# All six key copies of the head preparation on GpSimd, in a kernel of eight chained sublayers

## The chip, the cores and the metric

One core of one Trainium2 chip runs the whole program in one launch. The time is the device time of that core in microseconds. Before the change its median is 3116.63 us over three runs, from 3113.25 to 3116.71.

## The reference

The input is 2 x 1024 tokens of width 128. Four layers follow, each an attention part and a feed-forward part, and around each part there is a layer norm before, a layer norm after and a residual add. The change touches the second part only, `_L0_ffn_ref`, which is 16-head attention of head width 8 plus a mixture of eight experts:

```
qkv = (x @ W_qkv + b_qkv).reshape(B, S, 3, H, hd)          # H = 16, hd = 8, S = 1024
q, k, v = (qkv[:, :, 0], qkv[:, :, 1], qkv[:, :, 2])
attn = jnp.einsum('bqhd,bkhd->bhqk', q, k) / jnp.sqrt(jnp.asarray(hd, x.dtype))
attn = jax.nn.softmax(attn, axis=-1)
attn_out = jnp.einsum('bhqk,bkhd->bqhd', attn, v).reshape(B, S, D)
gate = jax.nn.softmax(x @ W_gate + b_gate, axis=-1)
...
return attn_out + moe_out
```

## The kernel before

The program is a row of phases, one behind another. Each phase is a block with one instruction list for each engine, and engines meet only at semaphores inside a block and at its end. The eight sublayers run in order, with a norm phase between them.

The part concerned is the phase `hprep` (lines 727 to 838), which prepares the 16-head attention of width 8. It works on 16 tiles (g = 0 to 15) of 128 tokens. To get products of float32 quality from bf16 operands, every query and key is split into three bf16 parts: `split3` (L703) casts to `hi`, subtracts, casts to `mid`, subtracts, casts to `lo`. These are five DVE instructions, L705 to L709, and each waits on the one before it through the semaphore `chain`. Keys go into `kstack`, where each head has 64 slots; six of its blocks of eight hold the parts in the order hi, mid, hi, mid, lo, hi. Queries go into `qstack` in another order. Then `kstack` is turned, so that head width lies on partitions.

For each tile the engines do this:

- TensorE (PE): the projection of tile g into one of two PSUM banks (L768, waits until DVE has read tile g-2 from that bank), then `turn(g-2)`: eight transposes of `kstack` (L755), which wait for `stack_act`, `stack_pool`, `stack_dve` and, through `turn_kept`, for ACT to have emptied the same half of the PSUM tile.
- DVE: bias added to q and k (L821, reads PSUM and `bias`) and to v (L823, the same), the five steps of `split3`, then `sem_inc(parts_done)`, which releases ACT and GpSimd. Then DVE itself copies the last three of the six key blocks into `kstack` (L837).
- GpSimd (POOL): the first three of the six key blocks (L805), after `parts_done` and after the transposes of the tile two back.
- ACT: six copies of query parts into `qstack` (L781), then for the tile two back the move of the turned keys from PSUM into `kT` (L786).

`kstack`, `qk`, `parts` and both PSUM tiles have two buffers, taken in turn. `rest` has one. The order on each engine is the order in which the code is written; there is no planner. After `hprep` the phase `heads` (L840 on) computes scores, softmax and values of the same attention; it begins once all engines have left `hprep`.

Of the kernel before, what the change touches and what calls it, by code (L numbers as in the profile page):

```python
# [23 lines left out]
P = 128  # L24
# [341 lines left out]
def load_weights(sp, m, dram, s):  # L366

    if s < len(PACKS):
        at = s % 2 * WPART[0]
        sp.dma_start(m.weights[:, at:at + WIDTHS[s]], dram[f"w{s}"]).then_inc(m.wsem[s], 16)  # L370
# [326 lines left out]

SLOTS = 64
BUFS = 10
POOL_SLOTS = 3  # L700


def split3(nc, chain, src, hi, mid, lo, rest):  # L703

    chain.step(nc.vector.tensor_copy(hi, src))  # L705
    chain.step(nc.vector.tensor_tensor(rest, src, hi, ALU.subtract))
    chain.step(nc.vector.tensor_copy(mid, rest))
    chain.step(nc.vector.tensor_tensor(rest, rest, mid, ALU.subtract))
    chain.step(nc.vector.tensor_copy(lo, rest))  # L709


def small_head_attention(nc, m, dram, s, router):
# [7 lines left out]
    with ExitStack() as keep:  # L720
# [6 lines left out]
        with Phase(nc, "hprep") as ph:  # L727
            kstack = ph.sb("kstack", [P, 2, 16, SLOTS], BF16)
            qk = ph.sb("qk", [P, 2, 256])
            parts = ph.sb("parts", [P, 2, 3, 256], BF16)  # L730
            rest = ph.sb("rest", [P, 256])
            bias = ph.sb("bias", [P, 384])
            proj = ph.ps("proj", 2)
            turned = ph.ctx.enter_context(nc.psum_tensor("hprep_turned", [P, 2, 1024], BF16))
            cleared, proj_done, qk_done, v_done, parts_done, chain_sem, stack_act, stack_pool, stack_dve, turn_done, turn_kept, bias_done, bias_kept = (
                ph.sem(x) for x in ("cleared", "proj_done", "qk_done", "v_done", "parts_done", "chain", "stack_act",
                                    "stack_pool", "stack_dve", "turn_done", "turn_kept", "bias_done", "bias_kept"))
            block = ph.block()

            @block.sync  # L740
            def _(sp):
                load_weights(sp, m, dram, s + 1)

            @block.tensor
            def _(pe):
                pe.wait_ge(m.wsem[s], 16)

                def turn(g):
                    pe.wait_ge(stack_act, g + 1)
                    pe.wait_ge(stack_pool, g + 1)  # L750
                    pe.wait_ge(stack_dve, g + 1)
                    if g >= 2:
                        pe.wait_ge(turn_kept, g - 1)
                    for c in range(8):
                        last = nc.tensor.transpose(turned[:, g % 2, c * P:(c + 1) * P],  # L755
                                                   kstack[:, g % 2, 2 * c:2 * c + 2, :].rearrange("p h d -> p (h d)"),
                                                   m.identb[:])
                    last.then_inc(turn_done, 1)

                nc.tensor.matmul(proj[:, 1, 0:384], m.ones[0:1, :], w["bqkv"], start=True,  # L760
                                 stop=True).then_inc(bias_done, 1)
                for g in range(NT):
                    if g == 1:
                        pe.wait_ge(bias_kept, 1)
                    if g >= 2:
                        pe.wait_ge(qk_done, g - 1)
                        pe.wait_ge(v_done, g - 1)
                    nc.tensor.matmul(proj[:, g % 2, 0:384], m.HT[:, g * P:(g + 1) * P], w["Wqkv"], start=True,  # L768
                                     stop=True).then_inc(proj_done, 1)
                    if g >= 2:  # L770
                        turn(g - 2)
                turn(NT - 2)
                turn(NT - 1)

            @block.scalar
            def _(act):
                def stack(g):
                    act.wait_ge(parts_done, g + 1)
                    hi, mid, lo = (parts[:, g % 2, k, 0:P].rearrange("p (h d) -> p h d", h=16) for k in range(3))
                    for slot, part in enumerate((hi, hi, mid, mid, hi, lo)):  # L780
                        last = nc.scalar.activation(qstack[:, g, :, 8 * slot:8 * slot + 8], part, ACT.Copy)  # L781
                    last.then_inc(stack_act, 1)

                def keep_turned(g):
                    act.wait_ge(turn_done, g + 1)
                    nc.scalar.activation(kT[:, :, g * P:(g + 1) * P], turned[:, g % 2, :].rearrange("p (c n) -> p c n", c=8),  # L786
                                         ACT.Copy).then_inc(turn_kept, 1)
                act.wait_ge(cleared, 5)
                for g in range(NT):
                    stack(g)  # L790
                    if g >= 2:
                        keep_turned(g - 2)
                keep_turned(NT - 2)
                keep_turned(NT - 1)

            @block.gpsimd
            def _(pool):
                pool.wait_ge(cleared, 5)
                for g in range(NT):
                    pool.wait_ge(parts_done, g + 1)  # L800
                    if g >= 2:
                        pool.wait_ge(turn_done, g - 1)
                    hi, mid, lo = (parts[:, g % 2, k, P:2 * P].rearrange("p (h d) -> p h d", h=16) for k in range(3))
                    for slot, part in enumerate((hi, mid, hi, mid, lo, hi)[:POOL_SLOTS]):
                        last = nc.gpsimd.tensor_copy(kstack[:, g % 2, :, 8 * slot:8 * slot + 8], part)  # L805
                    last.then_inc(stack_pool, 1)

            @block.vector
            def _(dve):
                chain = Chain(dve, chain_sem)  # L810
                nc.vector.memset(kstack[:, :, :, 51:64], 0.0).then_inc(cleared, 1)
                nc.vector.memset(kstack[:, :, :, 48:51], 1.0).then_inc(cleared, 1)
                nc.vector.memset(qstack[:, 0:8, :, 48:64], 0.0).then_inc(cleared, 1)
                nc.vector.memset(qstack[:, 8:16, :, 48:64], 0.0).then_inc(cleared, 1)
                nc.vector.memset(vaug[:, :, :, 8], 1.0).then_inc(cleared, 1)
                dve.wait_ge(bias_done, 1)
                nc.vector.tensor_copy(bias[:], proj[:, 1, 0:384]).then_inc(bias_kept, 1)
                dve.wait_ge(bias_kept, 1)
                for g in range(NT):
                    dve.wait_ge(proj_done, g + 1)  # L820
                    nc.vector.tensor_tensor(qk[:, g % 2, :], proj[:, g % 2, 0:256], bias[:, 0:256],  # L821
                                            ALU.add).then_inc(qk_done, 1)
                    nc.vector.tensor_tensor(vaug[:, g, :, 0:8], proj[:, g % 2, 256:384].rearrange("p (h d) -> p h d", h=16),  # L823
                                            bias[:, 256:384].rearrange("p (h d) -> p h d", h=16),
                                            ALU.add).then_inc(v_done, 1)
                    dve.wait_ge(qk_done, g + 1)
                    if g >= 2:
                        dve.wait_ge(stack_act, g - 1)
                        dve.wait_ge(stack_pool, g - 1)
                    split3(nc, chain, qk[:, g % 2, :], parts[:, g % 2, 0, :], parts[:, g % 2, 1, :],  # L830
                           parts[:, g % 2, 2, :], rest[:])
                    dve.sem_inc(parts_done, 1)
                    if g >= 2:
                        dve.wait_ge(turn_done, g - 1)
                    hi, mid, lo = (parts[:, g % 2, k, P:2 * P].rearrange("p (h d) -> p h d", h=16) for k in range(3))
                    for slot, part in list(enumerate((hi, mid, hi, mid, lo, hi)))[POOL_SLOTS:]:
                        last = nc.vector.tensor_copy(kstack[:, g % 2, :, 8 * slot:8 * slot + 8], part)  # L837
                    last.then_inc(stack_dve, 1)

        with Phase(nc, "heads") as ph:  # L840
            qT = ph.sb("qT", [P, 2, 8, P], BF16)
# [49 lines left out]
            slot = {e: k % 2 for k, e in enumerate(RING)}  # L891
# [366 lines left out]
def attention_and_top2(nc, m, dram, s):  # L1258
    with ExitStack() as keep:
        router = Router(nc, keep)  # L1260
        small_head_attention(nc, m, dram, s, router)
        top2_experts(nc, m, dram, s, router)
# [2610 lines left out]
```

## Time and profile before

| | |
|---|---|
| median of three runs | 3116.63 us |
| the profiled execution, its own time | 3116.61 us |
| span of its trace | 3114.8 us |
| stretch from 238 to 287 us (nearly all of the 16 tiles of `hprep`) | 49 us |
| in it DVE busy | 44.38 us |
| in it PE busy | 32.11 us |
| in it ACT busy | 32.09 us |
| in it POOL busy | 11.79 us |

The profile shows one execution. The span runs from its first to its last recorded instruction; 1.81 us of the run lie outside it. A row of the timeline gives the start in us, the time from start to end in us, the engine, the line, the operation with output and input, how many instructions are merged in the row, and in brackets how long the engine had stood idle and who released it. Instructions of one engine that do not wait for each other overlap in the records, so three of 0.29 us can take 0.76 us together. The profile of a kernel of 3 ms must be read by stage: `hprep` is 1.6% of it.

### The profile page before, as it was taken

The numbers are of one execution on the slowest core, as the hardware profiler recorded it, in microseconds if no ns is written. First come the engines' busy times: TensorE is split into PE (matmuls) and PEld (weight loads), VectorE is DVE, ScalarE is ACT, GpSimd is POOL, SyncE is SP. The second block draws the span as 40 slices with busy tenths as digits, with TensorE's granted clock in tenths as the row PEclk, the third lists the DMA queues.
The fourth block names the chain that finished last, engine by engine and source line by source line (L and its number), as shares of the span: only waits on it lengthen the run. The fifth ranks groups of instructions, "written<-read, shape, count | busy, mean of one in ns | idle before, by whom it ended". The sixth has DMA issues, their size and how long they took to land. (4 is left out here: it accounts for less than half of the span.)

```text
span 3114.8 us, 55189 instructions
## 1 busy us (share of the span) xinstructions
PE 2705.1 (87%) x21256; PEld 1691.7 (54%) x21276; DVE 2057.1 (66%) x4308; ACT 1571.8 (50%) x3080; POOL 1074.1 (34%) x784
## 2 busy tenths in 40 slices
PE   8995899989899799998999798798877899777698
PEld 5552455567676566665567566465643334335465
DVE  5758999945644665647554665466548999996554
ACT  4334688862423444444544555365457676643122
POOL 3201000001143344434443444154227777773000
PEclk9995899989899899999999899998999999998899
DMA  1000000001120200000000000000013344340000
GB/s 55 1 4 1 2 3 3 3 2 61 49 92 22 84 1 1 1 1 1 1 1 1 29 1 1 1 1 1 1 52 135 136 143 143 137 141 27 1 1 14
DMA packets 34228, 105.41 MB, mean 34 GB/s; under 512 B 3456, under 2 KB 14592, under 8 KB 33200
## 3 DMA queue, kind: packets, MB, share of 16 engines
q1 hardware_dynamic: 31952, 97.69, 9.0%
q0 software_dynamic: 2016, 4.19, 0.4%
q8 instruction: 171, 2.80, 0.4%
q14 instruction: 89, 0.73, 0.1%
HBM read 94.01 MB, written 7.86 MB: 33 GB/s over the span
## 5 line engine op out<-in xcount | busy, mean ns | idle before, releaser
L2082 POOL TENSOR_TENSOR many_probs<-many_probs,many_rinv 128x2048 f32<-128x2048 f32 (+7 forms) x128 | 269.8, 2107 | 371.6 <-DVE many_rinv L2121 371.6
L1062 DVE TENSOR_REDUCE heads_halfmax<-heads_qmajor 128x1 f32<-128x512 f32 x512 | 316.4, 681 | 32.8 <-PE heads_qmajor L923 29.4
L3477 DVE TENSOR_TENSOR_SCAN stream_state<-stream_decay,stream_state 128x512 f32<-128x512 f32 x256 | 306.3, 1233 | 0.8 <-ACT stream_decay L3309 0.5
L1027 ACT ACTIVATE weights<-heads_kmajor 128x1024 f32<-128x1024 f32 x256 | 259.3, 1027 | 71.7 <-PE heads_kmajor L935 66.3
L2051 ACT ACTIVATE many_probs<-many_score,many_negmax 128x1024 f32<-128x1024 f32 (+7 forms) x256 | 187.4, 737 | 179.7 <-DVE many_negmax L2105 175.9
L2105 DVE TENSOR_REDUCE many_negmax<-many_score 128x1 f32<-128x1024 f32 (+7 forms) x256 | 184.4, 751 | 110.4 <-PE many_score L1980 108.9
L3147 PE MATMUL stream_yacc<-stream_state,ident 128*128 128x512 f32 x512 | 249.1, 614 | 0.4 <-POOL stream_state L3439 0.4
L3309 ACT ACTIVATE stream_decay<-weights,mamba_negA 128x512 f32<-128x512 f32 x256 | 173.0, 689 | 112.5 <-DVE stream_state L3477 111.3
L3439 POOL TENSOR_TENSOR stream_state<-XN,stream_state 128x1024 f32<-128x1024 f32 x85 | 200.4, 2360 | 81.4 <-DVE stream_state L3477 81.1
L1988 PE MATMUL many_ring<-ident,many_probs 128*128 128x128 f32 x1152 | 177.4, 282 | 28.1 <-POOL many_probs L2082 6.5
L3468 DVE TENSOR_TENSOR stream_state<-stream_bspread,stream_du 128x1024 f32<-128x1024 f32 x128 | 153.2, 1197 | 46.5 <-POOL stream_du L3415 38.6
L2041 ACT ACTIVATE many_probsT<-many_ring 128x512 f32<-128x512 f32 x192 | 107.7, 561 | 143.8 <-PE many_ring L1988 143.6
L1988 PEld LDWEIGHTS many_ring<-ident,many_probs 128*128 128x128 f32 x1152 | 127.4, 142 | 91.9 <-DVE many_zT L2115 34.7
L951 PE MATMUL heads_outp<-weights,heads_vaug 128*9 128x128 f32 x4096 | 161.2, 276 | 13.5 <-ACT heads_outT L1020 13.2
L2004 PE MATMUL many_ring<-many_probsT,many_v 128*64 128x128 f32 x2304 | 154.1, 278 | 13.8 <-ACT many_probsT L2041 12.2
L2467 ACT ACTIVATE local_probs<-local_score,local_negmax,loc_norms 128x192 f32<-128x192 f32 x256 | 127.3, 507 | 68.0 <-DVE local_negmax L2482 67.9
L1976 PE MATMUL many_score<-many_kT,many_qT 64*128 64x512 f32 (+3 forms) x768 | 159.8, 520 | 1.2 <-ACT many_probs L2051 1.2
L3147 PEld LDWEIGHTS stream_yacc<-stream_state,ident 128*128 128x128 f32 x512 | 101.2, 198 | 90.0 <-issue 71.8
L3138 PE MATMUL stream_bspread<-stream_BC,stream_select 128*128 128x512 bf16 x236 | 76.2, 399 | 81.8 <-DVE stream_state L3468 74.2
L2004 PEld LDWEIGHTS many_ring<-many_probsT,many_v 128*64 128x64 f32 x2304 | 123.2, 137 | 33.9 <-ACT many_probsT L2041 20.2
L2519 POOL TENSOR_TENSOR local_probs<-local_probs,local_rowsum 128x768 f32<-128x768 f32 x64 | 93.9, 1467 | 137.3 <-DVE local_rowsum L2488 137.3
L184 POOL TENSOR_TENSOR norm_rstd<-norm_rstd,neghalf 128x4 f32<-128x4 f32 x46 | 46.8, 1016 | 263.7 <-DVE norm_rstd L178 263.7
(585 smaller groups left out, 6023.7 us busy)
## 6 DMA issues: line engine op xcount, KB each, us to landing
XN<-mamba_crows SPq DMA_DIRECT2D x85, 512.0 KB, 3.6
stream_crow<-mamba_crows SPq DMA_DIRECT2D x43, 512.0 KB, 3.6
weights<-in_w_dram SPq DMA_DIRECT2D x1, 6148.0 KB, 17.8
weights<-in_w_dram SPq DMA_DIRECT2D x1, 4274.0 KB, 12.8
weights<-in_w_dram SPq DMA_DIRECT2D x1, 3296.0 KB, 10.7
swiglu_pairs<-swiglu_fetched SPq DMA_DIRECT2D x1, 2310.0 KB, 10.2
weights<-in_w_dram SPq DMA_DIRECT2D x1, 2112.0 KB, 7.9
swiglu_fetched<-swiglu_pairs SPq DMA_DIRECT2D x4, 528.0 KB, 7.3
```

The lines of the kernel that those rows point to most:

```text
L951: last = nc.tensor.matmul(outp[32 * j:32 * j + 9, 0, c * P:(c + 1) * P], vaug[:, b * TPB + kc, 4 * c + j, :], probs_of(4 * q + j // 2 * 2 ...
L1027: nc.scalar.activation(probs_of(k).rearrange("p (a n) -> p a n", a=2), kmajor[:, at:at + 2, :], ACT.Exp, scale=SC).then_inc(exp_done, 1)
L1062: nc.vector.tensor_reduce(halfmax[:, g % 2, at, h % 2:h % 2 + 1], qmajor[:, (2 * n + j) % 3, :], AX, ALU.max).then_inc(max_done, 1)
L1988: last = nc.tensor.transpose(ring[:, k % 2, x % 4 * P:(x % 4 + 1) * P], probs[:, n % 4, x * P:(x + 1) * P], m.ident[:])
L2004: last = nc.tensor.matmul(ring[DH * h:DH * (h + 1), k % 2, 0:P], v[:, g % 2, kb, DH * h:DH * (h + 1)], probsT[:, n % 2, x * P:(x + 1) * P] ...
L2051: nc.scalar.activation(probs[:, n % 4, h * wide:(h + 1) * wide], score_of(n, h)[:, 0:wide], ACT.Exp, bias=negmax[:, n % 3, h:h + 1], accum ...
L2082: nc.gpsimd.tensor_tensor(pair, pair, rinv[:, n % 4, :].unsqueeze(2).broadcast_to([P, 2, wide]), ALU.mult).then_inc(norm_done, 1)
L2105: nc.vector.tensor_reduce(negmax[:, n % 3, h:h + 1], score_of(n, h)[:, 0:(UNITS[n][1] + 1) * P], AX, ALU.max, negate=True).then_inc(negmax ...
L3147: last = nc.tensor.matmul(yacc[:, half, :], m.ident[:], state[:, g % STATES, part(half)], start=(g % NS == 0), stop=(g % NS == NS - 1))
L3309: nc.scalar.activation(decay[:, h % DECAYS, :], delta_of(j, ch)[:, part(half)], ACT.Exp, scale=negA[:, a:a + 1]).then_inc(dec_done, 1)
L3439: nc.gpsimd.tensor_tensor(state[:, g % STATES, :], crow_of(g), state[:, g % STATES, :], ALU.mult).then_inc(hc_done, 1)
L3477: nc.vector.tensor_tensor_scan(h[:, part(half)], decay[:, (2 * g + half) % DECAYS, :], h[:, part(half)], 0.0 if half == 0 else h[:, BANK - ...
```

## The change

All six key blocks are copied by GpSimd. DVE goes from `sem_inc(parts_done)` straight to the next tile. The semaphore `stack_dve`, PE's wait for it and DVE's wait for `turn_done` go with the DVE copies.

```
--- before.py
+++ after.py
@@ -697,7 +697,6 @@
 
 SLOTS = 64
 BUFS = 10
-POOL_SLOTS = 3
 
 
 def split3(nc, chain, src, hi, mid, lo, rest):
@@ -732,9 +731,9 @@
             bias = ph.sb("bias", [P, 384])
             proj = ph.ps("proj", 2)
             turned = ph.ctx.enter_context(nc.psum_tensor("hprep_turned", [P, 2, 1024], BF16))
-            cleared, proj_done, qk_done, v_done, parts_done, chain_sem, stack_act, stack_pool, stack_dve, turn_done, turn_kept, bias_done, bias_kept = (
+            cleared, proj_done, qk_done, v_done, parts_done, chain_sem, stack_act, stack_pool, turn_done, turn_kept, bias_done, bias_kept = (
                 ph.sem(x) for x in ("cleared", "proj_done", "qk_done", "v_done", "parts_done", "chain", "stack_act",
-                                    "stack_pool", "stack_dve", "turn_done", "turn_kept", "bias_done", "bias_kept"))
+                                    "stack_pool", "turn_done", "turn_kept", "bias_done", "bias_kept"))
             block = ph.block()
 
             @block.sync
@@ -748,7 +747,6 @@
                 def turn(g):
                     pe.wait_ge(stack_act, g + 1)
                     pe.wait_ge(stack_pool, g + 1)
-                    pe.wait_ge(stack_dve, g + 1)
                     if g >= 2:
                         pe.wait_ge(turn_kept, g - 1)
                     for c in range(8):
@@ -801,7 +799,7 @@
                     if g >= 2:
                         pool.wait_ge(turn_done, g - 1)
                     hi, mid, lo = (parts[:, g % 2, k, P:2 * P].rearrange("p (h d) -> p h d", h=16) for k in range(3))
-                    for slot, part in enumerate((hi, mid, hi, mid, lo, hi)[:POOL_SLOTS]):
+                    for slot, part in enumerate((hi, mid, hi, mid, lo, hi)):
                         last = nc.gpsimd.tensor_copy(kstack[:, g % 2, :, 8 * slot:8 * slot + 8], part)
                     last.then_inc(stack_pool, 1)
 
@@ -830,12 +828,6 @@
                     split3(nc, chain, qk[:, g % 2, :], parts[:, g % 2, 0, :], parts[:, g % 2, 1, :],
                            parts[:, g % 2, 2, :], rest[:])
                     dve.sem_inc(parts_done, 1)
-                    if g >= 2:
-                        dve.wait_ge(turn_done, g - 1)
-                    hi, mid, lo = (parts[:, g % 2, k, P:2 * P].rearrange("p (h d) -> p h d", h=16) for k in range(3))
-                    for slot, part in list(enumerate((hi, mid, hi, mid, lo, hi)))[POOL_SLOTS:]:
-                        last = nc.vector.tensor_copy(kstack[:, g % 2, :, 8 * slot:8 * slot + 8], part)
-                    last.then_inc(stack_dve, 1)
 
         with Phase(nc, "heads") as ph:
             qT = ph.sb("qT", [P, 2, 8, P], BF16)
```

What GpSimd's list holds per tile is afterwards: wait `parts_done`, wait `turn_done` (from the third tile on), six copies, of which the last signals `stack_pool`. Nothing else in the program is changed.

## Rows read from the trace of the kernel before

**Rows 1.** The page: span, and busy time of each engine with share and count.
```profile
span 3114.8 us, 55189 instructions
PE 2705.1 (87%) x21256; PEld 1691.7 (54%) x21276; DVE 2057.1 (66%) x4308; ACT 1571.8 (50%) x3080; POOL 1074.1 (34%) x784
```

**Rows 2.** Stretch, length, busy (count) of PE, PEld, DVE, ACT, POOL; clock, DMA share, GB/s.
```profile
238.00:287.00 49.00, 32.11 (x146) 17.57 (x146) 44.38 (x151) 32.09 (x109) 11.79 (x47) 0.53 0.00 1
```

**Rows 3.** Timeline, DVE, one steady tile, to the next tile's first instruction.
```profile
260.68 0.41 DVE L821 TENSOR_TENSOR hprep_qk<-hprep_proj,hprep_bias 128x256 f32<-128x256 f32 x1
...
261.21 0.28 DVE L705 CAST hprep_parts<-hprep_qk 128x256 bf16<-128x256 f32 x1
261.52 0.43 DVE L706 TENSOR_TENSOR hprep_rest<-hprep_qk,hprep_parts 128x256 f32<-128x256 f32 x1
261.98 0.29 DVE L707 CAST hprep_parts<-hprep_rest 128x256 bf16<-128x256 f32 x1
262.31 0.43 DVE L708 TENSOR_TENSOR hprep_rest<-hprep_rest,hprep_parts 128x256 f32<-128x256 f32 x1
262.77 0.29 DVE L709 CAST hprep_parts<-hprep_rest 128x256 bf16<-128x256 f32 x1
263.21 0.79 DVE L837 COPY hprep_kstack<-hprep_parts 128x128 bf16<-128x128 bf16 x3
263.91 0.41 DVE L821 TENSOR_TENSOR hprep_qk<-hprep_proj,hprep_bias 128x256 f32<-128x256 f32 x1
```

**Rows 4.** Timeline, the other engines in the same tile.
```profile
259.92 1.30 ACT L781 ACTIVATE heads_qstack<-hprep_parts 128x128 bf16<-128x128 bf16 x6 [1.02 <-DVEq L832]
261.13 1.00 ACT L786 ACTIVATE heads_kT<-hprep_turned 128x1024 bf16<-128x1024 bf16 x1
...
263.18 0.76 POOL L805 COPY hprep_kstack<-hprep_parts 128x128 bf16<-128x128 bf16 x3 [2.47 <-DVEq L832]
...
262.28 1.01 PE L755 MATMUL hprep_turned<-identb,hprep_kstack 128*128 128x128 bf16 x8 [0.84 <-ACT heads_kT L786]
263.08 1.59 PE L768 MATMUL hprep_proj<-weights,HT 128*128 128x384 f32 x2
```

**Rows 5.** Timeline, first tile's hand-over, and end of the phase.
```profile
237.51 0.63 DVE L837 COPY hprep_kstack<-hprep_parts 128x128 bf16<-128x128 bf16 x3
237.56 0.76 POOL L805 COPY hprep_kstack<-hprep_parts 128x128 bf16<-128x128 bf16 x3 [10.49 <-DVEq L832]
238.05 0.41 DVE L821 TENSOR_TENSOR hprep_qk<-hprep_proj,hprep_bias 128x256 f32<-128x256 f32 x1
...
285.79 1.30 ACT L781 ACTIVATE heads_qstack<-hprep_parts 128x128 bf16<-128x128 bf16 x6 [1.02 <-DVEq L832]
...
288.14 1.01 PE L755 MATMUL hprep_turned<-identb,hprep_kstack 128*128 128x128 bf16 x8 [2.22 <-ACT heads_kT L786]
```

**Rows 6.** Copies into `kstack`, whole trace: shortest, median and longest in ns.
```profile
L837 DVE COPY hprep_kstack<-hprep_parts x48: 194/320/321, 237.5 to 286.3; 128x128 bf16<-128x128 bf16 x48
L805 POOL COPY hprep_kstack<-hprep_parts x48: 288/293/295, 237.6 to 286.3; 128x128 bf16<-128x128 bf16 x48
```

**Rows 7.** Timeline of the first sublayer, DVE and POOL beside each other.
```profile
57.22 2.36 POOL L607 TENSOR_TENSOR lin_keytotal<-lin_keytotal,lin_key 128x1024 f32<-128x1024 f32 x1 [2.36 <-DVE lin_key L623]
59.01 1.12 DVE L628 SCALAR_TENSOR_TENSOR lin_qry<-lin_featexp,lin_featrelu 128x512 f32<-128x512 f32 x1 [1.87 <-ACT lin_featrelu L577]
61.14 0.69 DVE L628 SCALAR_TENSOR_TENSOR lin_qry<-lin_featexp,lin_featrelu 128x512 f32<-128x512 f32 x1 [0.42 <-ACT lin_featrelu L577]
...
138.31 0.88 DVE L212 TENSOR_TENSOR X<-X,XN 128x128 f32<-128x128 f32 x4
138.47 2.94 POOL L607 TENSOR_TENSOR lin_keytotal<-lin_keytotal,lin_key 128x1024 f32<-128x1024 f32 x1 [2.63 <-DVE lin_key L623]
```

**Rows 8.** Timeline of the Mamba stage, POOL and DVE beside each other.
```profile
2398.12 2.36 POOL L3439 TENSOR_TENSOR stream_state<-XN,stream_state 128x1024 f32<-128x1024 f32 x1 [1.06 <-DVE stream_state L3477]
2399.01 1.20 DVE L3468 TENSOR_TENSOR stream_state<-stream_bspread,stream_du 128x1024 f32<-128x1024 f32 x1
```

More of the change, by code:

```diff
@@ L699 @@
 BUFS = 10
-POOL_SLOTS = 3
 def split3(nc, chain, src, hi, mid, lo, rest):
@@ L734, in small_head_attention @@
             turned = ph.ctx.enter_context(nc.psum_tensor("hprep_turned", [P, 2, 1024], BF16))
-            cleared, proj_done, qk_done, v_done, parts_done, chain_sem, stack_act, stack_pool, stack_dve, turn_done, turn_kept, bias_done, bias_kept = (
+            cleared, proj_done, qk_done, v_done, parts_done, chain_sem, stack_act, stack_pool, turn_done, turn_kept, bias_done, bias_kept = (
                 ph.sem(x) for x in ("cleared", "proj_done", "qk_done", "v_done", "parts_done", "chain", "stack_act",
-                                    "stack_pool", "stack_dve", "turn_done", "turn_kept", "bias_done", "bias_kept"))
+                                    "stack_pool", "turn_done", "turn_kept", "bias_done", "bias_kept"))
             block = ph.block()
@@ L750, in turn @@
                     pe.wait_ge(stack_pool, g + 1)
-                    pe.wait_ge(stack_dve, g + 1)
                     if g >= 2:
@@ L803, in _ @@
                     hi, mid, lo = (parts[:, g % 2, k, P:2 * P].rearrange("p (h d) -> p h d", h=16) for k in range(3))
-                    for slot, part in enumerate((hi, mid, hi, mid, lo, hi)[:POOL_SLOTS]):
+                    for slot, part in enumerate((hi, mid, hi, mid, lo, hi)):
                         last = nc.gpsimd.tensor_copy(kstack[:, g % 2, :, 8 * slot:8 * slot + 8], part)
@@ L832, in _ @@
                     dve.sem_inc(parts_done, 1)
[L833 to L838, printed above, removed]
         with Phase(nc, "heads") as ph:
```

## The prediction

> **What bounds the kernel now.** The page comes first. PE is busy for 87% of the span, DVE for 66%, POOL for 34% [rows 1]. That would make PE the limit and a change on DVE worthless, but it is an average over eight sublayers with different limits. So the second look goes to the stage that is changed. From 238 to 287 us DVE is busy for 44.38 of 49 us, PE and ACT for 32.1 each, POOL for 11.8 [rows 2]. Here DVE is the limit, and POOL has three quarters of its time free.
>
> The third look is the timeline, to see whether DVE ever waits for another engine. One tile takes from 260.68 to 263.91, that is 3.23 us, and in it DVE has no idle time that a row names [rows 3]. ACT waits 1.02 us in each tile and POOL 2.47 us, both for DVE's `parts_done` [rows 4]. PE waits 0.84 us for ACT [rows 4], and ACT waited for DVE. The loop from tile to tile is thus DVE's own instruction list: two bias adds, five dependent steps, three copies.
>
> **What is removed.** The three copies L837 start at 263.21 and the next tile's L821 at 263.91: 0.70 us of DVE's list per tile [rows 3]. In the first hand-over it is 238.05 - 237.51 = 0.54 us [rows 5]. There are 15 hand-overs between 16 tiles. After the last tile nothing on DVE follows, and what ends the phase is ACT and PE, below. If nothing else moved, the gain would be 14 x 0.70 + 0.54 = 10.3 us, with 3.23 - 0.70 = 2.53 us per tile. DVE's wait for `turn_done` and PE's wait for `stack_dve` go too; both hang on work that other waits already cover (POOL waits for the same `turn_done`, PE for `stack_pool`), so I count them at nothing.
>
> **What is added on POOL.** Three copies take 0.76 us and one alone 0.293, so they start 0.235 us apart [rows 4, 6]. Six take 0.293 + 5 x 0.235 = 1.47 us. POOL has 3.23 - 0.76 = 2.47 us free now and would still have 1 us free at 2.53 us per tile. Behind the copies on POOL's queue there are only the next tile's copies.
>
> **Who waits for POOL's last copy.** `turn(g)` on PE does. I set time 0 at the DVE instruction that follows `sem_inc` (263.21 in the trace). POOL starts at -0.03 and would end at 1.44. ACT starts `stack(g)` at -0.06; in the trace its keep of tile g-2 begins 261.13 - 259.92 = 1.21 us later and takes 1.00, so it ends at 2.15. PE starts 0.15 us after that (262.13 to 262.28), at 2.30 [rows 4]. So the transposes wait for ACT's `turn_kept` anyway, and POOL may be 0.8 us later than 1.44 before anybody sees it.
>
> **What is late next.** PE needs 263.08 - 262.28 = 0.80 us for the transposes and 1.59 us for the projection: 2.39 us per tile [rows 4], at a granted clock of 0.53 in this stretch [rows 2]. ACT needs 1.21 + 1.00 = 2.21 us [rows 4]. Both lie under 2.53. The projection for tile g+3 ends at 2.30 + 0.80 + 1.59 = 4.69, and DVE asks for it at two tiles, 5.06. It is in time by 0.37 us. If PE lost the 0.15 us of its hand-over in every tile, its loop would be 2.54 us; this costs 0.01 us a tile. DVE stays the limit, with PE close behind.
>
> **The collision.** This is the term that isn't plain. POOL's copies used to run beside DVE's own copies. Now they run beside the next tile's L821, L823, L705, L706, L707. Does DVE slow down beside POOL? The trace has cases.
> - L837 took 194 ns at the shortest, 320 in the median [rows 6]. The short ones are in the first tile, where DVE started 0.05 us ahead of POOL [rows 5]. In the later tiles POOL starts 0.03 us ahead (263.18, 263.21) [rows 3, 4], and each DVE copy takes 0.126 us longer. POOL's stay at 288 to 295 ns.
> - A DVE instruction with two SBUF inputs, L628, starts at 59.01 beside a POOL instruction that ends at 57.22 + 2.36 = 59.58. It takes 1.12 us in place of 0.69, so its work began at 60.13 - 0.69 = 59.44, which is 0.14 us before POOL's record ends [rows 7].
> - The other way round, POOL's L607 at 138.47 takes 2.94 us in place of 2.36. It was held until 139.05, and the DVE instructions beside it end at 138.31 + 0.88 = 139.19, again 0.14 us later [rows 7].
> - A DVE instruction that reads PSUM and SBUF, L3468, runs in the middle of a POOL instruction, from 2399.01 within 2398.12 to 2400.48, and is done at 2400.21, before POOL's ends [rows 8]. It can't have been held off. L821 and L823 are of that kind.
>
> So I read it as exclusion: each holds the other off from its start until 0.14 us before its record ends. For a POOL copy this is 0.293 - 0.14 = 0.153 us. A DVE copy that starts 0.03 us later should wait 0.12, and 0.126 was measured.
>
> The Trainium skill (SBUF — State Buffer, section Who interferes with whom) says that DVE and GpSimd lock the pair of SBUF ports that they share, that DVE needs it for a fast copy or cast between SBUF tensors and against GpSimd's reads for two SBUF inputs, and that whichever issues second is blocked for the whole of the first one's instruction. It is a rule against this change. By whole records it gives the slower rival below (3120.8 us); the trace agrees with the exclusion and puts its end 0.14 us ahead of the record's.
>
> Now step by step, with starts from rows 3 relative to L821 (L705 at 0.53, L706 0.84, L707 1.30, L708 1.63, L709 2.09). POOL's copies start at -0.03, 0.205, 0.44, 0.675, 0.91, 1.145. L821 and L823 are not held. L705 at 0.53 meets the third copy, which holds until 0.593: a wait of 0.063. From there the two take turns. L705 holds until 0.73, and the fourth copy goes then, until 0.883. L706 is ready at 0.903 and holds until 1.19. The fifth copy holds until 1.343, and L707 is ready at 1.363 and holds until 1.52. The sixth holds until 1.67, and L708 is ready at 1.693. After each DVE step there are 0.14 + 0.035 us in which DVE uses nothing, and a POOL copy needs 0.153 of them. So DVE loses 0.063 us per tile, and POOL ends at 1.81, still before 2.15. I take 0.063, by [rows 6, 7]. The bounds: below, 0 (no meeting at all); above, L705 to L708 each wait the measured 0.126, that is 0.50 us. A gain from contention is excluded, since nothing of POOL's is taken away beside L705 to L709.
>
> **Sum.** 2.53 + 0.063 = 2.59 us per tile. 14 x (0.70 - 0.063) = 8.9, and in the first hand-over 0.54 - 0.063 = 0.48: 9.4 us. The end of the phase keeps its form: ACT's last stack at 285.79, PE's last transposes at 288.14 after two keeps [rows 5]; POOL's last copies, 1.47 us from 285.8, end by 287.3 and hide under it. The profiled execution took 3116.61 us, its span 3114.8 [rows 1], with 1.81 us around it; it is 0.02 us off the median of 3116.63. So 3116.61 - 9.4 = 3107.2 us.
>
> **Rivals.**
> - *Every step of DVE waits.* The 0.02 us of spare between a POOL copy and the next DVE step is thin. If all four of L705 to L708 wait 0.126 us, a tile saves 0.20 us, the first hand-over 0.04: 2.8 us, 3113.8. With three waits it is 14 x 0.32 + 0.16 = 4.7 us, 3111.9. I take 3112 for this case. For it: each of the three copies in a tile waits, not just the first [rows 6]. Against: those don't wait for each other, while L705 to L709 leave gaps.
> - *Given back later.* `heads` begins 9 us earlier, and PE's clock changes at other moments; it is 0.53 on average in this stretch [rows 2], and PE is the busiest engine of the whole [rows 1]. The three runs before differ by 3.5 us. If as much is lost, it is about 3110.7. Nothing in the profile says which way, so the chance is small.
> - *Slower.* POOL and DVE exclude each other for their whole records and alternate. L705 waits from 0.53 until the third copy's end at 0.733 (0.20); L706, L707 and L708 each wait for a whole copy less the gap between steps (0.293 - 0.035 = 0.258). Together 0.97 us, 0.27 more than the 0.70 removed, in the first hand-over 0.43 more: 14 x 0.27 + 0.43 = +4.2 us, 3120.8. It decides from 0.175 us per step on. Against it: 0.14 us in two places [rows 7], and a DVE and a POOL copy that fit together into 0.235 us.
>
> **How the numbers follow.** Forecast 0.55, every step waits 0.28, given back 0.10, slower 0.07. What a measurement of this kernel can tell from no change is about 0.2%, 6.2 us. The forecast is a gain of 9.4 us, or 0.30%, and passes it unless 3 us go astray (0.93). Of the second case a fifth passes, of the third half: 0.51 + 0.06 + 0.05, rounded down to 0.60, since the model of the collision is mine. The slower rival ends 0.13% above and passes 0.2% less than half the time; with what I have not thought of, 0.06. The rest, 0.34, is no measurable change. The range: below, 3106.3 with no meeting at all and 2 us of the runs' spread, 3104.5; above, 3113.8 and a little, 3114.5. Outside it is mostly the slower rival.
>
> **What the changed profile would show.** No L837 on DVE; L821 0.44 us after the start of L709; 96 POOL copies. L821 to L821 2.59 us. L705 about 0.34 us in place of 0.28 [rows 3], L706 to L708 as before within 0.03. POOL copies no longer all 293 ns but up to some 0.52 (the one held by L706). PE's transposes still released by ACT's L786. Steady stretch about 9 us shorter, everything behind it shifted and unchanged. I am wrong if L706 to L708 lengthen by 0.1 or more (second case), if PE waits for POOL's L805 or DVE for L768 (a limit that I put below DVE), or if the stretch shrinks by 9 us and the run doesn't.

## The result

Over eight runs each, the changed kernel takes 3104.40 us in the median (3101.22 to 3109.48) and the kernel before 3112.41 us (3110.42 to 3116.71). The ratio is 0.9975, 95% interval 0.9964 to 0.9985: 4.7 to 11.2 us faster. A second comparison with more runs gives 0.9979 (0.9970 to 0.9988). The forecast was 9.4 us faster and 3107.2 us. The median of 3104.40 lies 0.1 us below the lower end of the stated range, 3104.5, because the median of the kernel before is itself 4.2 us lower over eight runs than over the three that the range started from. The profiled execution of the changed kernel took 3103.46 us.

The page of the changed kernel, its first two lines (span; busy time of each engine, share, count). They answer to [rows 1]:

```profile
span 3101.6 us, 55173 instructions
PE 2694.6 (87%) x21256; PEld 1686.0 (54%) x21276; DVE 2046.6 (66%) x4260; ACT 1573.1 (51%) x3080; POOL 1091.6 (35%) x832
```

The shares say nothing of the change; the counts do: 48 instructions fewer on DVE, 48 more on POOL.

The steady stretch by windows (length, then busy us of PE, PEld, DVE, ACT, POOL, granted clock, DMA, GB/s), answering to [rows 2]:

```profile
236.00:274.00 38.00, 23.70 (x139) 13.38 (x138) 33.96 (x103) 30.66 (x103) 27.43 (x90) 0.79 0.00 1
```

DVE is busy for 89% of it (91% before), ACT now for 81%, POOL for 72%. DVE is still the limit. Lines move by one to two in the changed file: L821 before is L819 after, L823 is L821, L705 to L709 are L704 to L708, L805 is L803, L755 is L753, L786 is L784.

Timeline of DVE in one steady tile of the changed kernel, to be laid beside [rows 3]:

```profile
254.08 0.42 DVE L819 TENSOR_TENSOR hprep_qk<-hprep_proj,hprep_bias 128x256 f32<-128x256 f32 x1
254.42 0.28 DVE L821 TENSOR_TENSOR heads_vaug<-hprep_proj,hprep_bias 128x128 f32<-128x128 f32 x1
254.62 0.35 DVE L704 CAST hprep_parts<-hprep_qk 128x256 bf16<-128x256 f32 x1
255.00 0.43 DVE L705 TENSOR_TENSOR hprep_rest<-hprep_qk,hprep_parts 128x256 f32<-128x256 f32 x1
255.46 0.29 DVE L706 CAST hprep_parts<-hprep_rest 128x256 bf16<-128x256 f32 x1
255.79 0.43 DVE L707 TENSOR_TENSOR hprep_rest<-hprep_rest,hprep_parts 128x256 f32<-128x256 f32 x1
256.25 0.29 DVE L708 CAST hprep_parts<-hprep_rest 128x256 bf16<-128x256 f32 x1
256.69 0.42 DVE L819 TENSOR_TENSOR hprep_qk<-hprep_proj,hprep_bias 128x256 f32<-128x256 f32 x1
```

A tile takes 256.69 - 254.08 = 2.61 us where it took 3.23. The three copies are gone, and of the seven instructions that are left one is longer by more than 0.01 us: the first cast, 0.35 us in place of 0.28.

The other engines in the same stretch, answering to [rows 4]:

```profile
254.05 1.85 POOL L803 COPY hprep_kstack<-hprep_parts 128x128 bf16<-128x128 bf16 x6 [0.76 <-DVEq L830]
...
254.02 1.30 ACT L779 ACTIVATE heads_qstack<-hprep_parts 128x128 bf16<-128x128 bf16 x6 [0.40 <-DVEq L830]
...
253.77 0.61 PE L753 MATMUL hprep_turned<-identb,hprep_kstack 128*128 128x128 bf16 x8 [1.30 <-ACT heads_kT L784]
254.22 0.86 PE L766 MATMUL hprep_proj<-weights,HT 128*128 128x384 f32 x2
...
258.99 1.01 PE L753 MATMUL hprep_turned<-identb,hprep_kstack 128*128 128x128 bf16 x8 [0.21 <-ACT heads_kT L784]
259.80 1.59 PE L766 MATMUL hprep_proj<-weights,HT 128*128 128x384 f32 x2
```

POOL's six copies take 1.85 us, not the 1.47 of six undisturbed ones, and it still waits 0.76 us for DVE in each tile. PE is released by ACT's L784 as before, never by POOL in the steady part. Two tiles of PE stand there because its clock changed in between: 0.61 and 0.86 us at the higher level, 1.01 and 1.59 at the lower. At the lower one PE's spare time is 0.21 us a tile.

The spread of the casts and the copies over all 16 tiles of the changed kernel (ns shortest, median, longest), the copies answering to [rows 6]:

```profile
L704 DVE CAST hprep_parts<-hprep_qk x16: 281/347/417, 233.8 to 272.9; 128x256 bf16<-128x256 f32 x16
L705 DVE TENSOR_TENSOR hprep_rest<-hprep_qk,hprep_parts x16: 424/425/426, 234.1 to 273.3; 128x256 f32<-128x256 f32 x16
L803 POOL COPY hprep_kstack<-hprep_parts x96: 290/298/521, 235.8 to 276.1; 128x128 bf16<-128x128 bf16 x96
```

From the first bias add to the start of the last cast `hprep` takes 41.3 us (233.2 to 274.5), where it took 50.4 (235.0 to 285.4): 9.1 us less. The rest of the difference between the two profiled executions, 13.15 - 9.1 = 4.0 us, lies outside `hprep` and is dealt with below.

### The profile page after: what moved, and what is told of

Same layout as the page of the kernel before. It is cut to its first block and busy times, and to the rows that moved or that the text cites. A ratio compares the mean times of both kernels' runs of the same rounds, so it can differ in the third digit from the quotient of the medians.

```text
span 3101.6 us, 55173 instructions
## 1 busy us (share of the span) xinstructions
PE 2694.6 (87%) x21256; PEld 1686.0 (54%) x21276; DVE 2046.6 (66%) x4260; ACT 1573.1 (51%) x3080; POOL 1091.6 (35%) x832
```

## The experiments

My theory: DVE's instruction list sets the tile. POOL and DVE exclude each other at SBUF from an instruction's start until 0.14 us before its record ends. Of POOL's copies only the third costs DVE anything, because it is under way when the first cast starts; the later ones slip into the gaps between DVE's dependent steps. The rivals: each POOL copy costs DVE a share; PE, ACT or POOL sets the tile; the kernel gains behind `hprep`.

**E1, three copies left out.** Not shown in the cut: the blocks that nobody copies now are cleared once, ahead of the first tile.

```
-for slot, part in enumerate((hi, mid, hi, mid, lo, hi)):
+for slot, part in enumerate((hi, mid, hi, mid, lo, hi)[:3]):
```

> The changed kernel, but GpSimd copies only the first three of the six key blocks; the other three are left out (kstack is cleared once, about 1 us ahead of the first tile). Theory (exclusion: DVE's cast of q and k meets only the GpSimd copy that is running when the cast starts, the third, and loses 0.07 us): the cast L705 stays at 0.35 us, since the third copy is still there, and a tile takes 2.61 us as with six copies. Rival (each GpSimd copy costs DVE something): half the copies, half the loss, 0.31 us for the cast or 2.57 us a tile. Second rival (a tile is set by PE, ACT or GpSimd, not by DVE's list): the period falls or stays whatever the cast does; GpSimd's end no longer matters.

**E2, four copies left out.** The same with `[:2]`.

> The same with only two of the six key blocks copied, the other four left out. Theory: the second GpSimd copy is over 0.17 us before the cast starts, so the cast takes 0.276 us and a tile 2.54 us, the whole step from 2.61 at once between three copies and two. Rival (each copy costs a share): 0.30 us and 2.56 us.

The first cast and POOL's copies, first in E1:

```profile
L803 POOL COPY hprep_kstack<-hprep_parts x48: 289/293/296, 238.5 to 278.0; 128x128 bf16<-128x128 bf16 x48
L704 DVE CAST hprep_parts<-hprep_qk x16: 282/346/416, 236.4 to 275.5; 128x256 bf16<-128x256 f32 x16
```

and in E2:

```profile
L803 POOL COPY hprep_kstack<-hprep_parts x32: 289/293/295, 236.7 to 275.1; 128x128 bf16<-128x128 bf16 x32
L704 DVE CAST hprep_parts<-hprep_qk x16: 282/283/285, 234.7 to 272.9; 128x256 bf16<-128x256 f32 x16
```

With three copies fewer the cast is as long as with all six, 346 to 347 ns. With one fewer again it drops to 283 ns at once, and a tile goes from 2.61 to 2.55 us (251.96 to 254.51, 257.05). So it is the third copy. The fourth to sixth cost DVE nothing (E1 against the changed kernel), and the first two at most the 7 ns between this cast's 276 ns in the kernel before and its 283 here. The share rival is out. E1 took 3109.62 us and E2 3104.11 in their one run each; the times can't tell that apart, the rows can.

**E3, eight copies on POOL**, the two added ones into a tile that nobody reads.

```
 for slot, part in enumerate((hi, mid, hi, mid, lo, hi)):
-    last = nc.gpsimd.tensor_copy(kstack[...], part)
+    nc.gpsimd.tensor_copy(kstack[...], part)
+for slot, part in enumerate((hi, mid)):
+    last = nc.gpsimd.tensor_copy(spare[...], part)
```

> The changed kernel with two more GpSimd copies per tile, into a tile that nobody reads, so that GpSimd has eight. Theory: the seventh and eighth fall into the gaps between DVE's steps; no DVE instruction becomes longer, a tile stays at 2.61 us, GpSimd's copies of one tile last about 2.4 us in place of 1.85, and PE, which needs them at 2.3 us after parts_done, waits for GpSimd by 0.1 to 0.2 us without DVE noticing, because the projection is early by 0.37 us. Rival (each copy costs DVE 0.07 to 0.13 us): 2.75 to 2.87 us a tile, L708 or L709 longer. Rival (GpSimd or PE is already as good as the limit): over 2.7 us a tile, DVE waiting for PE or for stack_pool.

The spread in E3, then one tile's rows on POOL and PE:

```profile
L806 POOL COPY hprep_spare<-hprep_parts x32: 293/379/516, 239.0 to 278.0; 128x128 bf16<-128x128 bf16 x32
L704 DVE CAST hprep_parts<-hprep_qk x16: 284/345/416, 235.2 to 274.3; 128x256 bf16<-128x256 f32 x16
L707 DVE TENSOR_TENSOR hprep_rest<-hprep_rest,hprep_parts x16: 424/426/426, 236.3 to 275.5; 128x256 f32<-128x256 f32 x16
...
252.88 1.85 POOL L804 COPY hprep_kstack<-hprep_parts 128x128 bf16<-128x128 bf16 x6
254.68 0.84 POOL L806 COPY hprep_spare<-hprep_parts 128x128 bf16<-128x128 bf16 x2
...
253.01 0.95 PE L754 MATMUL hprep_turned<-identb,hprep_kstack 128*128 128x128 bf16 x8 [0.21 <-POOL hprep_spare L806]
```

A tile still takes 2.61 us (252.91 to 255.52), and no DVE instruction is longer. POOL is now busy without a pause, 1.80 + 0.81 = 2.61 us a tile, and PE does wait for it. Eight copies just fit. Two numbers of my expectation were too low. POOL's copies of a tile last 2.6 us, where I had 2.4. And PE starts its transposes 253.01 - 250.31 = 2.70 us after the first add of the tile before, where the changed kernel has 253.77 - 251.47 = 2.30: PE is held 0.40 us, not 0.1 to 0.2. The one run took 3108.32 us. One term of the prediction is seen best here: what DVE doesn't pay, POOL pays. Six copies are stretched by 0.38 us (1.85 in place of 1.47), two by 0.31.

**E4, the kernel before with DVE's copies ahead of the signal.**

```
+[wait turn_done, three copies into kstack, inc stack_dve]
 dve.sem_inc(parts_done, 1)
-[wait turn_done, three copies into kstack, inc stack_dve]
```

> The kernel before, with DVE's three copies moved ahead of sem_inc(parts_done), so that GpSimd's three start after them. Theory (who starts first holds the other off): DVE's copies take 0.194 us each and start 0.18 us apart in place of 0.320 and 0.235, GpSimd's three then run beside the next tile's L821 to L705, whose cast becomes 0.35 us, and a tile takes 3.23 - 0.16 + 0.07 = 3.14 us. Rival (a DVE copy of this form takes 0.32 us in steady state whatever GpSimd does): copies stay at 0.32 us and a tile takes 3.23 us or more.

The spread, then one tile of DVE and POOL in E4:

```profile
L836 DVE COPY hprep_kstack<-hprep_parts x48: 187/195/302, 235.7 to 278.4; 128x128 bf16<-128x128 bf16 x48
...
252.38 0.29 DVE L709 CAST hprep_parts<-hprep_rest 128x256 bf16<-128x256 f32 x1
252.71 0.50 DVE L836 COPY hprep_kstack<-hprep_parts 128x128 bf16<-128x128 bf16 x3
253.13 0.41 DVE L821 TENSOR_TENSOR hprep_qk<-hprep_proj,hprep_bias 128x256 f32<-128x256 f32 x1
...
252.81 0.82 POOL L805 COPY hprep_kstack<-hprep_parts 128x128 bf16<-128x128 bf16 x3 [2.01 <-DVEq L838]
```

The first two of the three copies take 195 ns, as the theory said; the third starts at 252.92, behind POOL's first at 252.81, and takes 0.29. But a tile takes 2.83 us (253.13 to 255.96), not 3.14, and `hprep` 44.6 us: almost two thirds of the change's gain (5.8 of 9.1 us) with the copies still on DVE. Two things were missing in my sum. Copies that nothing holds start 0.10 to 0.11 us apart (252.71, 252.82, 252.92), not 0.18, and the signal costs DVE time of its own. In [rows 3] the first copy starts 0.44 us after the last cast starts, here 0.33: `sem_inc` stood between them and took 0.11 us. In E4 it passes through DVE's queue while the copies run: POOL is released at 252.81, with the last copy still to come. The copies and the signal together cost 0.33 + 0.42 = 0.75 us from cast to next add, against 0.44 + 0.70 = 1.14. And the cast stays at 0.28 us, since POOL's three copies start earlier against it.

In one tile of E4 POOL starts late, at 272.84 (why is not shown), and leaves DVE's copies alone:

```profile
272.55 0.40 DVE L836 COPY hprep_kstack<-hprep_parts 128x128 bf16<-128x128 bf16 x3
272.86 0.42 DVE L821 TENSOR_TENSOR hprep_qk<-hprep_proj,hprep_bias 128x256 f32<-128x256 f32 x1
273.40 0.35 DVE L705 CAST hprep_parts<-hprep_qk 128x256 bf16<-128x256 f32 x1
```

The three copies cost 0.31 us of DVE's list here, and the cast meets POOL's third copy again and takes 0.35. So of the 0.70 us of the kernel before more than half, 0.39, was the price of starting just behind POOL. The one run of E4 took 3107.92 us; the kernel before, run once beside E1 to E4, took 3117.43.

**E5, the last cast signals by itself**, on top of the change.

```
-split3(..., rest[:])
-dve.sem_inc(parts_done, 1)
+split3(..., rest[:], parts_done)   # its last cast: .then_inc(parts_done, 1), no wait after it
```

> The changed kernel, and the last cast of the split signals parts_done itself; DVE neither waits for it nor issues sem_inc. In the changed kernel the next tile's L819 starts 0.44 us after the last cast starts; without the wait it should start 0.20 us after it, as L704 does after L821. Theory (DVE's list sets the tile, PE is close behind): DVE's list becomes 2.61 - 0.24 = 2.37 us, and since DVE is now 0.12 us ahead of GpSimd's copies the cast meets none of them, 0.07 us less, 2.30 us. Then PE, 2.39 us at the lower clock, is the limit where the clock is low, and ACT, 2.21 us, is close: 2.3 to 2.4 us a tile, 3 to 4.5 us less than the changed kernel in all, 13 us less than before. Rival (the wait costs DVE nothing, since the next add would wait for the projection anyway): 2.61 us a tile, DVE idle behind PE.

DVE and ACT in one tile of E5, and between them PE and DVE in a later one:

```profile
251.83 0.29 DVE L709 CAST hprep_parts<-hprep_rest 128x256 bf16<-128x256 f32 x1
252.04 0.42 DVE L822 TENSOR_TENSOR hprep_qk<-hprep_proj,hprep_bias 128x256 f32<-128x256 f32 x1
...
252.57 0.29 DVE L704 CAST hprep_parts<-hprep_qk 128x256 bf16<-128x256 f32 x1
...
254.36 0.42 DVE L822 TENSOR_TENSOR hprep_qk<-hprep_proj,hprep_bias 128x256 f32<-128x256 f32 x1
...
259.78 1.59 PE L769 MATMUL hprep_proj<-weights,HT 128*128 128x384 f32 x2
261.09 0.29 DVE L709 CAST hprep_parts<-hprep_rest 128x256 bf16<-128x256 f32 x1
261.41 0.42 DVE L822 TENSOR_TENSOR hprep_qk<-hprep_proj,hprep_bias 128x256 f32<-128x256 f32 x1
...
252.16 1.31 ACT L782 ACTIVATE heads_qstack<-hprep_parts 128x128 bf16<-128x128 bf16 x6
253.37 1.00 ACT L787 ACTIVATE heads_kT<-hprep_turned 128x1024 bf16<-128x1024 bf16 x1
```

The add starts 0.21 us after the cast, the first cast takes 0.29 us, and a tile takes 2.32 us. That is DVE's own list: 2.61 less the 0.07 of the cast and the 0.23 of wait and signal is 2.31. ACT's rows in this tile no longer carry an idle time, so it is close, but nothing on DVE waits for it. PE was granted the higher clock in this stretch and waits 1.0 us a tile. At the lower clock it does become the limit, as expected: the projection that ends at 259.78 + 1.59 = 261.37 lets the next add start only at 261.41, 0.32 us after the last cast in place of 0.21, and that tile takes 2.43 us. Another one is delayed like it (2.49 us, projection until 240.37, add at 240.42), and in three more of the 15 the cast meets a POOL copy again (0.34 to 0.40 us). `hprep` is 37.4 us long. Over five runs the median is 3098.85 us (3097.42 to 3103.70), the ratio to the kernel before 0.9954 (0.9941 to 0.9968). It beats both kernels. Its median is 8.9 us below that of the changed kernel in the next comparison, though its `hprep` is only 3.9 us shorter; where the other 5 us come from no run shows.

**The two kernels again.** The changed kernel was run beside E5:

> The changed kernel again, as it is, beside the kernel before on the same chip. Theory: hprep is 9.1 us shorter as in its first profile (50.4 to 41.3 us from the first bias add to the start of the last cast), and the median is lower by 9 us with a spread of some 3 us; the 4 us more by which the two first profiled executions differ (1.7 us ahead of hprep, 2.3 us in the experts behind it) is spread between executions and not there in every profile. Rival (the changed kernel also gains behind hprep): the medians differ by 12 us or more.

Its median is 3107.77 us over 11 runs (3101.61 to 3109.22), that of the kernel before 3112.88 over 15 (3111.22 to 3118.98): 5 us apart, ratio 0.9979 (0.9970 to 0.9988), where I had expected 9; the interval reaches from 3.7 to 9.3 us. The kernel before got two more profiles:

> The kernel before, unchanged, for a second profile of it. hprep from first add to last cast is 50.4 us again. Theory (the differences outside hprep belong to single executions): the first add of hprep is not always at 235.0 but between 233 and 236 us, as it was in the seven profiles of other kernels, and the stretch from the heads' first scores to the single-head attention's first scores is not always 481.0 but in some profiles 479. Rival (the change shortens what follows it by 2.3 us): that stretch is 481 us in every profile of the kernel before.

> The kernel before, unchanged, for a third profile; the same expectations.

They took 3117.23 and 3116.90 us. Their first adds are at 233.4 and 235.3 us, and from the heads' first scores to the single-head attention's they take 478.9 and 480.9 us, where the first profile has 481.0: the kernel before has the shorter value too, as the theory wanted. The table gives, in us for each profiled execution, the time between the first instructions of chosen tiles: ahead of `hprep` (from the linear attention's second half to the first bias add), from the first bias add to the heads' first scores (`hprep` and its end), the experts with what surrounds them, and the two stretches behind.

| execution | ahead | hprep | experts to next scores | next | next |
|---|---|---|---|---|---|
| before | 153.7 | 57.6 | 75.0 | 129.6 | 149.9 |
| before, second | 151.6 | 57.6 | 72.0 | 132.1 | 151.7 |
| before, third | 153.6 | 57.7 | 75.0 | 129.6 | 149.9 |
| changed | 151.6 | 48.6 | 72.3 | 129.6 | 149.9 |
| changed, second | 153.8 | 48.5 | 72.3 | 129.6 | 150.3 |
| E5 | 151.5 | 44.6 | 71.9 | 132.3 | 151.5 |

Only the second column goes with the kernel: 9.0 to 9.1 us for the change, to 0.1 us in every pair. The others take, most of them, one of two values 2 to 3 us apart, and the kernel before has both. The heads' own stretch, left out of the table, takes 405.9 to 406.9 us in these six. In the experts' stretch it goes with PE's clock. The start of the experts by windows (columns as above), first profile of the kernel before:

```profile
698.00:708.00 10.00, 9.40 (x36) 7.54 (x36) 2.67 (x4) 0.55 (x1) 0.00 (x0) 0.54 0.00 0
708.00:718.00 10.00, 10.00 (x53) 7.58 (x53) 3.90 (x6) 0.00 (x0) 0.00 (x0) 0.77 0.01 2
```

and its second profile:

```profile
698.00:708.00 10.00, 10.00 (x46) 7.72 (x46) 3.36 (x5) 0.00 (x0) 0.00 (x0) 0.66 0.00 0
708.00:718.00 10.00, 10.00 (x68) 7.91 (x68) 6.46 (x17) 0.00 (x0) 1.01 (x1) 1.00 0.01 2
```

It is the same kernel; PE has no idle time in either from 708 to 718. Where the clock is already at 1.00 from 708 to 718 it gets 68 matmuls done in place of 53, and the stretch takes 72.0 us in place of 75.0. So the short stretch isn't peculiar to the changed kernel. But the rival that the change shortens what lies behind it is weakened by this, not out. Of ten profiles only two have the 75 us, and both are of the kernel before; the seven of kernels with a shorter `hprep` have 71.9 to 72.4. Over the last three columns the changed kernel takes 351.8 and 352.2 us, the kernel before 354.5, 355.8 and 354.5. Against the rival stand E1 and E3: their `hprep` is as short as the changed kernel's, and they take 355.2 and 355.1 us. From the heads' first scores to the last instruction the changed kernel takes 2819.8 and 2816.7 us, the kernel before 2822.1 to 2824.4, E1, E3 and E5 2823.3 to 2824.1.

## Why the prediction was right, step by step

- *What bounds it.* Right. DVE's list set the tile before, sets it after, and E1 and E3 change POOL's load and leave the tile at 2.61 us, while E2 (the cast), E4 and E5 change DVE's list and change the tile each time.
- *What is removed.* 0.70 us a tile, right. What I did not see is that 0.70 was the price of three copies that start just behind POOL's. E4 has them for 0.42, and for 0.31 in the tile where POOL stays clear of them. The prediction also calls the copies of the first tile the short ones; only the first of them takes 0.19 us, the other two 0.28 and 0.32.
- *POOL's copies, and who waits for them.* Right: PE is released by ACT. POOL ends at 254.05 + 1.85 - 254.08 = 1.82 us after DVE's first add; 1.81 was forecast.
- *What is late next.* PE's 2.39 us at the lower clock held, with 0.21 us to spare. What was not foreseen is that the clock rises within `hprep`: its mean from 236 to 274 us is 0.79 in place of 0.54, so PE was further from the limit than I put it. E5 shows what comes next: PE in tiles at the lower clock, and at the higher one still DVE's own list, with ACT close behind.
- *The collision.* Forecast: L705 waits 0.063 us, nothing else waits, a tile takes 2.59 us, POOL's longest copy is 0.52 us. Measured: 0.07 us, nothing else, 2.61 us, 0.521 us. The taking of turns came out as well: POOL's fourth to sixth copies, each held by one DVE step, take 0.35, 0.52 and 0.38 us. In the first tile POOL starts 0.05 us after DVE's add, not 0.03 before it, so the third copy stands later against the cast, and this cast took 0.417 us. I had put it in with the others; it costs 0.07 us in all.
- *The sum.* 9.4 us forecast, 9.1 in the profile of the stage. The 0.3 us are 14 times 0.01 to 0.02 and the longer cast in the first tile.
- *The time.* 3107.2 us forecast, 3104.40 and 3107.77 measured. The median difference is 8.0 us in the first comparison and 5.1 in the second; both intervals hold 9.1 us. The sum started from a profiled execution at 3116.61 us; the runs of the kernel before have their median 4 us lower, which I could not see from three runs.
- *The rivals.* That every step waits is out: L705 to L708 (after) are 424 to 426 and 293 to 295 ns. The slower one is out too, and with it the Trainium skill's wording (SBUF — State Buffer, section Who interferes with whom) that the second instruction is blocked for the whole of the first. The exclusion is real, but a POOL copy with a record of 0.293 us let DVE in after 0.153; by whole records the tile would have been 3.50 us.
- *Given back later* is not excluded by the medians. The profiles show no stage behind `hprep` that is longer by more than 0.3 us in the changed kernel than the kernel before has in one of its three; they show stages that take one of two durations. The profiled executions are not typical either: those of the two kernels differ by 13 to 16 us, the medians by 8.0 and 5.1. Whether the change alters how often each duration occurs is open, and so is why 5 to 8 us arrive in the medians and not 9.1. That the total came out within 2 us of 9.4 in the first comparison, and within 5 in the second, is in part luck; the 9.1 us of the stage are not.

## What to carry to other kernels

Moving work from an engine that sets a loop to an idle one is worth the list time that it frees, less what the two engines cost each other; lay out both lists on one time axis with their exclusions. For this change the answer came out to 0.02 us a tile; for E4 the same kind of sum missed by 0.31, because it had the spacing of the copies wrong and the signal at nothing. First ask whether the two engines merely start in a bad order: more than half of what the three copies cost DVE came from POOL starting 0.03 us ahead. Before moving work away, see how the loop signals: taking one wait and one `sem_inc` off DVE's list gained 3.9 us in `hprep` (41.3 to 37.4), on top of the 9.1 for three copies. In a kernel of 3 ms with a clock that changes, judge such a change by the length of its stage in the profile; the total moves by as much as the gain from one execution to the next (3101 to 3109 us for the changed kernel).

## What the runs showed of the hardware

- DVE and POOL exclude each other at SBUF from the start of an instruction to 0.14 us before its recorded end; this held for a 2.36 us POOL instruction, for four DVE adds [rows 7] and for copies of 0.293 us (E1, E2). A DVE instruction with one input in PSUM and one in SBUF was never held (L819, L821: 0.42 and 0.28 us in every tile, with POOL's copies beside them and in the first tile without).
- Three DVE copies of 128x128 bf16 with nothing of POOL's in their way start 0.10 to 0.11 us apart and take 0.31 us to the next add; started 0.03 us behind POOL's three they take 0.70 (E4, [rows 3]).
- A `sem_inc` of its own costs DVE 0.11 us between two instructions (0.44 against 0.33 us, E4), and the wait ahead of it another 0.12 (0.33 against 0.21, E5).
- PE's granted clock rose in the middle of `hprep` in the changed kernel: 0.50 from 232 to 242 us, with PE busy for 6.91 of these 10 us, and 1.00 from 242 to 252 (0.61 us for eight transposes at 2.4 GHz in place of 1.01 at 1.2). The kernel before had a mean of 0.54 from 236 to 274, and 0.50 from 250 to 260 with PE busy for 7.49 of 10 us. What raised it is not shown.
